# One piece of a last strip loaded by DMAs of 100 and 28 partitions, with a new cut of the last loads

## The reference

```python
keep = (u >= 0.1)
x_drop = x * keep / 0.9
y = x + jnp.matmul(adj, x_drop)          # adj 8192x8192, x 8192x64, all float32
m = jnp.mean(y, axis=-1, keepdims=True)
v = jnp.var(y, axis=-1, keepdims=True)
out = (y - m) / jnp.sqrt(v + 1e-5)
```

## Time and profile before

| what | value |
|---|---|
| median of 3 runs | 642.21 us (642.01 to 642.31) |
| profiled execution, its own time | 642.27 us |
| its span, first to last instruction | 640.5 us |
| mean rate of all DMAs over the span | 429 GB/s |
| TensorE matmul busy | 514.4 us, 80% |
| VectorE, ScalarE, GpSimd busy | 52.1, 10.8 and 18.0 us |
| mean granted TensorE clock | 0.924 of full |

### The profile page before, as it was taken

One profiled execution on the slowest core, in us unless ns is written; L12 is line 12 of the kernel. 1 busy time (PEld: TensorE's weight loads), 2 busy tenths in 40 slices (PEclk: granted clock), 3 DMA queues, 4 the chain that ended last, 5 costly groups with the idle time before them and its releaser, 6 DMA issues.

```text
span 640.5 us, 5695 instructions
## 1 busy us (share of the span) xinstructions
PE 514.4 (80%) x2308; PEld 176.1 (27%) x2308; DVE 52.1 (8%) x231; ACT 10.8 (2%) x18; POOL 18.0 (3%) x27
## 2 busy tenths in 40 slices
PE   0387797887977886887879869887887878888997
PEld 0122232232322322222222223222222222222335
DVE  3300101000010100001010010100001010000102
ACT  0000000000000000000000000000000000000000
POOL 0000000000000000000000000000000000000000
PEclk9999897988989899898889898898998888978999
DMA  9999999999999999999999999999999999999998
GB/s 391 427 435 439 429 425 443 417 438 429 434 431 456 424 434 440 430 427 443 411 443 425 430 436 452 415 450 440 426 431 437 417 443 421 434 432 434 429 421 349
DMA packets 9362, 274.83 MB, mean 429 GB/s; under 512 B 1168, under 2 KB 1424, under 8 KB 2448
## 3 DMA queue, kind: packets, MB, share of 16 engines
q1 hardware_dynamic: 9072, 274.63, 99.6%
q10 hardware_dynamic: 288, 0.16, 0.1%
HBM read 272.66 MB, written 2.13 MB: 429 GB/s over the span
## 4 chain that ended last, share of the span: by engine, by line
DMA 71%; PE 27%; issue 1%; DVE 0%; SPq 0%; POOL 0%; POOLq 0%; DVEq 0%
DMA raw<-adj_dram 71%; PE acc L162 26%; SPq L131 0%; PE turned L170 0%; POOL rstd L277 0%; PE final_acc L162 0%; DVE stats L247 0%; POOLq L45 0%; DVE rows L243 0%; SPq L134 0%; DVE moments L252 0%; POOLq L282 0%; DVE final_normed L270 0%; DVE var_eps L255 0%; DVEq L243 0%
## 5 line engine op out<-in xcount | busy, mean ns | idle before, releaser
L162 PE MATMUL acc<-raw,head 128*64 128x504 f32 x2048 | 488.1, 637 | 90.0 <-POOLq L282 89.8
L162 PEld LDWEIGHTS acc<-raw,head 128*64 128x64 f32 x2048 | 152.9, 148 | 413.5 <-issue 292.5
L243 DVE TENSOR_TENSOR rows<-turned,head 126x256 f32<-126x256 f32 x16 | 6.8, 425 | 540.1 <-PE turned L170 540.1
L277 POOL TENSOR_TENSOR rstd<-var_eps,minus_half 126x4 f32<-126x4 f32 x16 | 16.2, 1011 | 613.1 <-DMA raw<-adj_dram 394.3
L170 PE MATMUL turned<-join,sums 128*126 128x64 f32 x128 | 17.5, 279 | 10.2 <-ACT sums L219 10.2
L170 PEld LDWEIGHTS turned<-join,sums 128*126 128x126 f32 x128 | 15.3, 189 | 23.4 <-ACT sums L219 23.4
L219 ACT COPY sums<-acc 128x504 f32<-128x504 f32 x16 | 9.3, 578 | 615.7 <-PE acc L162 615.7
L258 DVE TENSOR_SCALAR normed<-rows,moments,rstd 126x64 f32 x64 | 15.7, 310 | 27.5 <-POOL rstd L277 27.5
L182 PE MATMUL final_turned<-head,eye 128*128 128x64 f32 x2 | 0.7, 448 | 21.3 <-DVE head L237 21.3
L247 DVE BATCH_NORM_STATS2 stats<-rows 126x6 f32<-126x64 f32 x64 | 9.7, 214 | 0.6
L162 PE MATMUL final_acc<-raw,head 128*64 128x128 f32 x124 | 7.7, 276 | 0.3 <-DMA raw<-adj_final_dram 0.2
(11 more groups left out here) (17 smaller groups left out, 3.5 us busy)
## 6 DMA issues: line engine op xcount, KB each, us to landing
raw<-adj_dram SPq DMA_DIRECT2D x30, 5544.0 KB, 26.7
raw<-adj_dram SPq DMA_DIRECT2D x15, 5040.0 KB, 29.2
raw<-adj_dram SPq DMA_DIRECT2D x2, 3024.0 KB, 21.2
raw<-adj_dram SPq DMA_DIRECT2D x2, 2520.0 KB, 26.8
head<-u_and_x_dram SPq DMA_DIRECT2D x1, 4128.0 KB, 13.7
raw<-adj_dram SPq DMA_DIRECT2D x1, 2016.0 KB, 20.6
out_dram<-normed SPq DMA_DIRECT2D x1, 1920.0 KB, 17.4
raw<-adj_dram SPq DMA_DIRECT2D x1, 1512.0 KB, 23.8
```

The lines of the kernel that those rows point to most:

```text
L162: last = nc.tensor.matmul(sum_bank[t * D:(t + 1) * D, 0:width], dropped[:, t * PAIRS + q, :], raw[:, s, start:start + width], start=(q == ...
L243: nc.vector.tensor_tensor(rows[:, :, :], turned[0:ROWS, 0:GROUPS, :], x_sb[0:ROWS, bass.ds(b * GROUPS, GROUPS), :], ALU.add).then_inc(turn ...
L277: nc.gpsimd.tensor_tensor(rstd[:, :], var_eps[:, :], minus_half[0:ROWS, :], ALU.pow).then_inc(rstd_ready, 1)
```

## The change

Four things are done to the lists of loads; no arithmetic on the data is changed.

1. `PARTS` has ten parts instead of eight. Slots 0 and 1 stay at 6 + 5 pairs each; slot 2 is cut into 3, 2, 2, 1, 1, 1 pairs instead of 4, 3, 2, 1. TensorE waits ten times in each block.
2. The last block but one (block 14) leaves SP's loop. Its slot 0 is one DMA, its slot 1 comes in two (6 + 5 pairs), its slot 2 in two (5 + 5 pairs), as the list `LOADS` says in numbers of parts. POOL passes each of them on by itself.
3. `FINAL` is cut as (23, 26), (26, 29) instead of (23, 27), (27, 29).
4. Piece number 4 of `FINAL`, pairs 23 to 25, is loaded by two DMAs, of partitions 0 to 99 and 100 to 127, on one semaphore; TensorE waits for the sum of both.

```diff
-PARTS = [..., (2, 22, 26), (2, 26, 29), (2, 29, 31), (2, 31, 32)]
+PARTS = [(0, 0, 6), (0, 6, 11), (1, 11, 17), (1, 17, 22), (2, 22, 25), (2, 25, 27), (2, 27, 29),
+         (2, 29, 30), (2, 30, 31), (2, 31, 32)]
+
+LOADS = [(2, 3), (3, 4), (4, 6), (6, 10)]
-FINAL = [(0, 4), (4, 12), (12, 18), (18, 23), (23, 27), (27, 29), (29, 31), (31, 32)]
+FINAL = [(0, 4), (4, 12), (12, 18), (18, 23), (23, 26), (26, 29), (29, 31), (31, 32)]
+UNEVEN = 4
+UNEVEN_ROWS = [(0, 100), (100, P)]
+FINAL_DMAS = [len(UNEVEN_ROWS) if n == UNEVEN else 1 for n in range(len(FINAL))]
...
-            def load_part(n):
-                s, q0, q1 = PARTS[n]
+            def load_parts(b, n0, n1):
+                s, q0, _ = PARTS[n0]
+                q1 = PARTS[n1 - 1][2]
                 q_slot = SLOT_PAIRS[s][0]
                 sp.dma_start(raw[:, s, (q0 - q_slot) * PAIR:(q1 - q_slot) * PAIR],
-                             adj[BLOCKS - 1, :, q0 * PAIR:q1 * PAIR]).then_inc(part_loaded[n], DMA)
+                             adj[b, :, q0 * PAIR:q1 * PAIR]).then_inc(part_loaded[n1 - 1], DMA)
...
-            with sp.Fori(1, BLOCKS - 1) as b:
+            with sp.Fori(1, BLOCKS - 2) as b:
...
+            sp.wait_ge(multiplied, (BLOCKS - 3) * SLOTS + 1)
+            load_slot(BLOCKS - 2, 0)
+            for n0, n1 in LOADS:
+                s, q0, _ = PARTS[n0]
+                if q0 == SLOT_PAIRS[s][0]:
+                    sp.wait_ge(multiplied, (BLOCKS - 3) * SLOTS + s + 1)
+                load_parts(BLOCKS - 2, n0, n1)
...
-                sp.dma_start(raw[:, 0, q0 * pair:q1 * pair],
-                             adj_final[:, q0 * pair:q1 * pair]).then_inc(final_loaded[n], DMA)
+                for p0, p1 in UNEVEN_ROWS if n == UNEVEN else [(0, P)]:
+                    sp.dma_start(raw[p0:p1, 0, q0 * pair:q1 * pair],
+                                 adj_final[p0:p1, q0 * pair:q1 * pair]).then_inc(final_loaded[n], DMA)
...
-                        pe.wait_ge(final_loaded[n], DMA)
+                        pe.wait_ge(final_loaded[n], FINAL_DMAS[n] * DMA)
...
-            def pass_part(n):
-                pool.wait_ge(part_loaded[n], DMA)
-                pool.sem_inc(landed, 1)
+            def pass_parts(n0, n1, loads):
+                pool.wait_ge(part_loaded[n1 - 1], loads * DMA)
+                pool.sem_inc(landed, n1 - n0)
...
-            for s in range(1, SLOTS):
-                pass_slot(BLOCKS - 2, s)
+            for n0, n1 in LOADS:
+                pass_parts(n0, n1, 1)
             for n in range(len(PARTS)):
-                pass_part(n)
+                pass_parts(n, n + 1, 2 if n + 1 in [n1 for _, n1 in LOADS] else 1)
```

More of the change, by code:

```diff
@@ L24 @@
 SLOT = max(q1 - q0 for q0, q1 in SLOT_PAIRS) * PAIR
-PARTS = [(0, 0, 6), (0, 6, 11), (1, 11, 17), (1, 17, 22), (2, 22, 26), (2, 26, 29), (2, 29, 31), (2, 31, 32)]
+PARTS = [(0, 0, 6), (0, 6, 11), (1, 11, 17), (1, 17, 22), (2, 22, 25), (2, 25, 27), (2, 27, 29),
+         (2, 29, 30), (2, 30, 31), (2, 31, 32)]
+LOADS = [(2, 3), (3, 4), (4, 6), (6, 10)]
 IN_SLOT = [sum(part[0] == s for part in PARTS) for s in range(SLOTS)]
-FINAL = [(0, 4), (4, 12), (12, 18), (18, 23), (23, 27), (27, 29), (29, 31), (31, 32)]
+FINAL = [(0, 4), (4, 12), (12, 18), (18, 23), (23, 26), (26, 29), (29, 31), (31, 32)]
+UNEVEN = 4
+UNEVEN_ROWS = [(0, 100), (100, P)]
+FINAL_DMAS = [len(UNEVEN_ROWS) if n == UNEVEN else 1 for n in range(len(FINAL))]
 P_DROP = 0.1
@@ L143, in _ @@
                     sp.wait_ge(multiplied, (BLOCKS - 2) * SLOTS + s + 1)
-                load_part(n)
+                load_parts(BLOCKS - 1, n, n + 1)
             sp.wait_ge(multiplied, (BLOCKS - 1) * SLOTS + 1)
```

## The result

The change makes the kernel slower: 643.37 us against 642.31, eleven runs each, +1.06 us; ratio 1.0022, 95% interval 1.0014 to 1.0031. I had forecast 641.7 with a range up to 643.1. The profiled execution took 643.43 us, its span is 641.6. Of the eleven times eight lie at 643.28 to 643.64 and three at 644.57 to 644.73; the kernel before has no such second group (642.01 to 642.45).

A forecast was written before the change was run, and what follows sets the result against it. DMA load bytes were taken to bound the kernel; splits +0.3, TensorE's end -0.19 and last store -0.55 to -0.6 made -0.5 us against the profiled 642.27, so a median of 641.7, range 641.2 to 643.1.

The forecast's parts named there:

- Piece 4, 100 and 28 partitions: Last strip's uneven load: ten engines get twelve rows, others two or none; an engine loses up to 0.91 us or gains 0.45.
- The loaded-engine rival: A late engine gets twelve rows of piece 4, delaying piece 5 and the stores: 642.95 us; chance 2.5 in 10.
- The splits: Four extra load DMAs in block 14 and the last block: +0.3 us on everything from piece 0 on, ends 0 and 0.6.
- the added waits: Two more TensorE waits in each of 16 blocks: no cost expected, covered by 89.8 us idle; uncovered, 1 us.
- The recut: Last strip, piece 4 three pairs instead of four: with late engines relieved, TensorE bound by itself from piece 3, 0.19 us won.
- The relief: Uneven piece 4 spares both late engines, so the last store ends with the others, 0.55 to 0.6 us sooner; 5 in 10.
- two late engines: Two of sixteen DMA engines run an estimated 1.2 to 1.7 us late at the end and set every landing.
- The cause of the lateness: Candidate at the start: an instruction fetch on q8 holds one engine 0.93 us, never regained while its queue is full.
- The sum: Whole kernel: splits +0.3, TensorE's end -0.19, last store -0.55 to -0.6, together -0.5 us; median 641.7.

The follow-up runs named there:

- run 13: Not a run label but a verb and a count: in the changed kernel TensorE does 13 pairs (pieces 3 to 6) without a wait.
- the uneven store: Kernel before, loads as they were; SP's store of blocks 12 to 14 cut into 100 and 28 partitions: 642.57 us against 642.25, ratio 1.0001.
- the uneven piece alone: Kernel before with only the new FINAL list and piece 4 in 100 and 28 partitions: 643.11 us against 642.34, +0.77.
- both stores: Kernel before; blocks 12 to 14 stored in 100 and 28 partitions, last block's store and last store in 119 and 9: 642.41 us against 642.38.
- the early pair: Kernel before; last pair of block 0's slot 2 loaded in 100 and 28 partitions, everything else as before: 645.45 us against 642.38.
- the 119 and 9: Kernel before; last block's store and last store cut into 119 and 9 partitions: 641.81 us against 642.25, -0.44, ratio 0.9993.

## Why the prediction was wrong

**What failed** is one step, under "Piece 4, 100 and 28 partitions": "A row of piece 4 is 3 KB; at 27 GB/s an engine [...] that is 0.113 us." I took the rate of whole 128-partition loads for DMAs of part of the partitions. In their place the runs showed 206 to 318 GB/s for some four microseconds, 0.67 MB or 1.6 us lost. The 3 KB rows of pieces 4 and 5 took a median of 0.20 us, against 0.125 with piece 4 whole. No rival held this. The loaded-engine rival (642.95) was near in time, but wrong in mechanism: with equal shares of 64 and 64 the kernel is slower still, +2.07.

**Where it struck** I had wrong as well. I had piece 4 land "hardly after piece 3"; so it did, because piece 3 itself came 1.76 us late. Engines that are done with piece 3 start on the uneven one while the late two still work on piece 3, so the slow rate falls on the landing that TensorE waits for. The packets bear this out: the thirteen slow rows are the last of piece 3, some six or seven for each late engine, and took 0.31 to 0.49 us instead of 0.20.

**The splits** were right: 0.3 us forecast, 0.19 at piece 0, 0.30 at piece 2 (630.84 against 630.54 in the trace of before), +0.26 for everything but the uneven piece. That is the whole of the splits, the added waits and the block 14 edit together; no run takes them apart. It leaves nothing that can be seen for the waits.

**The recut** (-0.19) can't be told apart from the splits in the kernel with piece 4 whole: L223 starts at 635.65 there against 635.29, 0.36 later, with piece 3 landing 0.37 later. I had counted the 0.19 as won only with both late engines relieved. In the changed kernel TensorE does run 13 pairs without a wait from piece 3, as forecast.

**The relief** was right in place and near in size: the last store lands 1.8 us after its issue, 2.2 before (-0.4, -0.55 forecast); 1.7 with the uneven store, 2.3 with 98 and 30. The reading of two late engines holds: in the kernel before fourteen engines end the block store at 637.3 to 638.05 us, the two others at 639.09 and 639.28, 1.0 and 1.2 us behind (1.2 to 1.7 estimated).

**The cause of the lateness** was a candidate in the prediction. No run moved the instruction fetch, but the packets of all 14 traces show it. In the kernel before the two 16 KB fetches run from 4.01 to 4.93 us and from 9.92 to 10.88. At the end of each starts one row of the first load that takes 1.7 us where its neighbours take 1.2, and the engine that carries it ends that load last or last but one. These two engines end the first load, at 13.97 us, 0.94 and 1.13 us after the fourteenth; at 620.68 us it is 1.06 and 1.26. Nothing in between gave it back.

**The sum** by measured terms: splits +0.2 to +0.3, slow rate +1.3 to +1.5 at the end of the matmuls (L223 +1.59 in all), last store -0.4: +1.2 measured in the profiled pair, where I had -0.5.

**What stays open** is the second group. Its times are 0.9 to 2.1 us higher; it was seen in the kernels with unequal shares (the change 3 of 11 times, the uneven piece alone 4 of 11, the uneven store 7 of 11, both stores 5 of 11, the early pair 4 of 5, the 119 and 9 alone 1 of 11) and neither in the kernel before nor in the three with equal shares (piece 4 whole, 64 and 64, 96 and 32). The six times with 98 and 30 are spread from 643.85 to 645.33 without clear groups. One engine late among the ten in some executions would explain the groups; that isn't shown. All eight profiles of kernels with groups fell in the first one. By the shares of the other executions (3, 4, 7, 1 and 5 of 10; the early pair left out) chance would do that about once in 200 times. So an execution with a profile seems to be no fair draw, and no trace here speaks for the second group.

## What to carry to other kernels

A load into part of the partitions is not a smaller load of the same rate: two DMAs of 64 partitions moved 211 GB/s where one of 128 moved 434, with the DMA engines fully busy in both, so look at GB/s and not at the busy share. Where the queue is full from end to end, move a relief of late engines behind the last load that anyone waits for, and take it from stores. Here that made the better executions 0.4 to 0.6 us shorter, of 642; only the 119 and 9 had ten of eleven times there, and even its interval doesn't exclude no change. Compare lists of times and not only medians when a deal depends on which engine does what, since a median can hide two groups.

## What was unexpected of the hardware

- Loads cut at partition 64 ran at 208 to 211 GB/s in steady state against 434 for whole ones; one 384 KB piece cut at 64, 96, 98 or 100 cost 0.8 to 1.8 us beside 642.60 for the same kernel with the piece whole, where 384 KB take 0.9 us at 429 GB/s.
- A cut slowed the load ahead of it in the queue: piece 3, itself of 128 partitions, began 1.76 us later.
- The store from SBUF cut at 100 lost nothing visible: 669 against 667 GB/s summed over the two microseconds from 636 on.
- Two 16 KB instruction fetches, at 4 and 10 us, each put one DMA engine about 1 us behind, and it was still as far behind at 621 us, with the queue full all the time (0.94 and 1.13 us at the first load's end, 1.06 and 1.26 at 620.68).
- These two engines end their share of the last store 0.5 us or so after the others in the kernel before; 100 and 28 partitions relieve both (it lands after 1.6 to 1.8 us), 98 and 30 or 64 and 64 don't (2.3 us).
